# Gathering and spreading the routed tokens in two fp32r passes, with the gates multiplied in later and two low parts made on GpSimd

## The reference

```python
gate_out = x @ gate_w + routing_bias
top_v, top_i = jax.lax.top_k(gate_out, K)                 # K = 4 of E = 16
chosen = jax.nn.one_hot(top_i, E, dtype=x.dtype).sum(axis=-2)
probs = jax.nn.softmax(jnp.where(chosen > 0, gate_out, NEG), axis=-1)
weights = probs * chosen
out = _swiglu(x, sw1, sw2, sw3)                            # a = x@w1; silu(a) * (x@w2) @ w3
for e in range(E):
    out = out + _swiglu(x, w1[e], w2[e], w3[e]) * weights[..., e:e + 1]
```

## Time and profile before

| what | value |
|---|---|
| median of three runs | 502.1 us |
| time of the profiled execution | 502.08 us |
| its span, first to last instruction | 500.3 us (1.8 us lie around it) |
| granted TensorE clock | 0.99 of full |
| PE busy | 483.9 us, 97% |
| VectorE, ScalarE, GpSimd busy | 272.4, 205.5 and 9.1 us |
| DMA | 191.05 MB, mean 382 GB/s; the large queue took 96.0% of the 16 engines' span |

### The profile page before, as it was taken

One profiled execution on the slowest core, in us unless ns is written; L12 is line 12 of the kernel. 1 busy time (PEld: TensorE's weight loads), 2 busy tenths in 40 slices (PEclk: granted clock), 3 DMA queues, 4 the chain that ended last, 5 costly groups with the idle time before them and its releaser, 6 DMA issues.

```text
span 500.3 us, 6706 instructions
## 1 busy us (share of the span) xinstructions
PE 483.9 (97%) x2596; PEld 309.9 (62%) x2596; DVE 272.4 (54%) x326; ACT 205.5 (41%) x227; POOL 9.1 (2%) x46
## 2 busy tenths in 40 slices
PE   8989799999999999999999999999999999999987
PEld 4755433447887666576666756656666676565554
DVE  6734530146889674466538357546555645753542
ACT  1110101035787264555435345455444535545320
POOL 2000000010100000000000000000000000000000
PEclk9989999999999899999999999999999999999999
DMA  8999999999986989999999999999999999999980
GB/s 335 422 420 421 423 419 420 417 419 409 414 357 232 374 279 351 412 417 400 373 417 416 356 417 415 374 404 417 415 364 415 416 363 417 415 398 373 418 327 23
DMA packets 37555, 191.05 MB, mean 382 GB/s; under 512 B 4218, under 2 KB 4602, under 8 KB 32148
## 3 DMA queue, kind: packets, MB, share of 16 engines
q1 hardware_dynamic: 37328, 190.48, 96.0%
q10 hardware_dynamic: 196, 0.14, 0.1%
HBM read 190.35 MB, written 0.26 MB: 381 GB/s over the span
## 4 chain that ended last, share of the span: by engine, by line
PE 84%; DMA 6%; DVE 6%; ACT 2%; issue 2%; POOL 0%; SPq 0%; ACTq 0%; DVEq 0%; POOLq 0%
PE ps L1712 15%; PE ps L1783 13%; PE ps L1726 13%; PE ps L1796 7%; PE ps L1716 7%; DMA w_raw<-in_w 6%; PE ps L1360 4%; PE ps L1524 3%; PE ps L1763 2%; PE ps L1553 2%; PE ps L1541 1%; PE ps L1353 1%; PE ps L1422 1%; PE ps L1438 1%; DVE s_lo L981 1%
## 5 line engine op out<-in xcount | busy, mean ns | idle before, releaser
L967 DVE TENSOR_TENSOR s_lo<-w_raw,s_hi 128x1365 fp32r<-128x1365 f32 x72 | 111.9, 1579 | 69.4 <-ACT s_hi L710 68.4
L710 ACT CAST s_hi<-w_raw 128x1365 fp32r<-128x1365 f32 x72 | 94.4, 1333 | 49.6 <-DMA w_raw<-in_w 48.1
L1712 PE MATMUL ps<-s_hi,xT_hi 128*128 128x512 f32 (+2 forms) x216 | 86.2, 399 | 2.1 <-DVE s_lo L967 2.1
L1712 PE MATMUL ps<-s_lo,xT_hi 128*128 128x512 f32 (+2 forms) x216 | 80.0, 372 | 0.0
L1726 PE MATMUL ps<-w_raw,exS 128*64 128x512 f32 x480 | 74.2, 455 | 0.0
L723 ACT CAST s_hi<-w_raw 128x1536 fp32r<-128x1536 f32 (+1 forms) x36 | 48.9, 1369 | 52.5 <-DMA w_raw<-in_w 51.8
L981 DVE TENSOR_TENSOR s_lo<-w_raw,s_hi 128x1536 fp32r<-128x1536 f32 (+1 forms) x36 | 57.7, 1619 | 2.3 <-ACT s_hi L723 2.0
L1726 PEld LDWEIGHTS ps<-w_raw,exS 128*64 128x64 f32 x480 | 33.2, 136 | 40.0 <-issue 40.0
L1716 PE MATMUL ps<-s_hi,xT_lo 128*128 128x512 f32 (+2 forms) x216 | 57.0, 372 | 0.0
L1712 PEld LDWEIGHTS ps<-s_hi,xT_hi 128*128 128x128 f32 x216 | 41.0, 190 | 21.4 <-issue 11.8
L1712 PEld LDWEIGHTS ps<-s_lo,xT_hi 128*128 128x128 f32 x216 | 41.1, 190 | 8.3 <-issue 1.9
(11 more groups left out here) (296 smaller groups left out, 449.0 us busy)
## 6 DMA issues: line engine op xcount, KB each, us to landing
w_raw<-in_w SPq DMA_DIRECT2D x128, 682.5 KB, 12.0
w_set<-in_w SPq DMA_DIRECT2D x31, 1024.0 KB, 24.6
w_raw<-in_w SPq DMA_DIRECT2D x27, 768.0 KB, 11.8
w_raw<-in_w3s SPq DMA_DIRECT2D x24, 768.0 KB, 12.1
w_raw<-in_sw SPq DMA_DIRECT2D x8, 682.5 KB, 15.7
w_raw<-in_w SPq DMA_DIRECT2D x9, 512.0 KB, 12.2
wk_sb<-in_wk SPq DMA_DIRECT2D x2, 1024.0 KB, 16.8
wq_sb<-in_wq SPq DMA_DIRECT2D x2, 1024.0 KB, 16.0
```

The lines of the kernel that those rows point to most:

```text
L710: a.copy(s_hi[pair_of(g)][:, 0:F1], raw[:, 0:F1]).then_inc(hi_ready, 1)
L967: v.tensor_tensor(s_lo[pair][:, 0:F1], raw[:, 0:F1], s_hi[pair][:, 0:F1].bitcast(F32), ALU.subtract).then_inc(lo_ready, 1)
L1712: mm(bank(i + c0 // D)[:, 0:n], xT_hi[:, k], w[:, c0:c0 + n], start=(k == 0 and w is hi), stop=False)
```

## The change

The matrices of zeros and ones are held in fp32r. The gather takes the tokens in a high part (`rows_hi`, ScalarE) and a low part (`rows_lo`, GpSimd), two fp32r matmuls in place of one of float32, and all four gathers stand after the third piece of w2. `plan_gates` is gone: `spread` is plain zeros and ones, a small set of matmuls (`gates_of_slots`) puts the gate of each place into a column, and the gating of a few step multiplies by it. A result `y` is added in a high and a low part (`y_to_hi` on ScalarE, `y_to_lo` on VectorE). In step 1 VectorE makes the low part of w2's piece 0 ahead of the plan, GpSimd those of pieces 1 and 2, VectorE that of piece 3 after the plan. The last few step keeps its float32 matmuls.

```diff
@@ gpsimd
+            def lo_of_w2(k):
+                g = unit_w2(1, k)
+                pool.wait_ge(hi_ready, g + 1)
+                pool.wait_ge(lo_ready, g)
+                hi, lo = s_hi[pair_of(g)], s_lo[pair_of(g)]
+                pg.tensor_tensor(lo[:, 0:F1], w2_raw[k][:, 0:F1], hi[:, 0:F1].bitcast(F32), ALU.subtract).then_inc(lo_ready, 1)
+
+            pool.wait_ge(rows_ready, 2)
+            pg.tensor_tensor(rows_lo[:], xn[:], rows_hi[:].bitcast(F32), ALU.subtract).then_inc(rows_ready, 1)
+            lo_of_w2(1)
+            lo_of_w2(2)
@@ scalar
+            def copy_gate_slot():
+                act.wait_ge(round_ps, KT + 3)
+                a.copy(gate_slot[:], bank(7)[:, 0:len(SPARSE)]).then_inc(gate_slot_ready, 1)
+
+            def y_to_hi(e):
+                act.wait_ge(raw_used, few_of[e, 2, W3_UNITS - 1] + 1)
+                if few_no(e) > 0:
+                    act.wait_ge(added, few_no(e))
+                a.copy(y_hi[:], bank(7)).then_inc(y_hi_ready, 1)
...
             a.activation(xn[:], x3[:], ACT.Copy, scale=rstd[:]).then_inc(rows_ready, 1)
+            act.wait_ge(rows_ready, 1)
+            a.copy(rows_hi[:], xn[:]).then_inc(rows_ready, 1)
             hT_to_hi(0, 2)
             hi_w2(1, 0)
             hi_w2(1, 1)
             silu(1)
             hi_w2(1, 2)
-            copy_gathered(0)
-            copy_gathered(1)
             hi_w2(1, 3)
-            copy_gathered(2)
-            copy_gathered(3)
+            for k in range(KT):
+                copy_gathered(k)
...
                     hi_w2(m, 2)
+                    y_to_hi(m - 1)
                     hi_w2(m, 3)
...
                         copy_spread(1)
+                        copy_gate_slot()
@@ vector
-                v.tensor_tensor(rows, act_a[:, 0:CW], few_row(NC), ALU.mult).then_inc(h_ready, 1)
-                v.tensor_copy(y_sb[:], bank(7)).then_inc(y_few_ready, 1)
+                v.scalar_tensor_tensor(rows, act_a[:, 0:CW], gate_slot[:, few_no(e):few_no(e) + 1], few_row(NC), ALU.mult, ALU.mult).then_inc(h_ready, 1)
+            def y_to_lo(e):
+                dve.wait_ge(y_hi_ready, few_no(e) + 1)
+                v.tensor_tensor(y_lo[:], bank(7), y_hi[:].bitcast(F32), ALU.subtract).then_inc(y_few_ready, 1)
...
             hT_to_lo(0, 2)
+            lo_w2(1, 0)
             plan_order()
             routed_gates()
-            lo_w2(1, 0)
-            lo_w2(1, 1)
             plan_tokens()
-            lo_w2(1, 2)
+            dve.wait_ge(lo_ready, unit_w2(1, 3))
             lo_w2(1, 3)
-            plan_gates()
...
-                    copy_y(m - 1)
                     lo_w2(m, 2)
+                    y_to_lo(m - 1)
                     lo_w2(m, 3)
@@ tensor
-                mm(bank(6), spread[:, few_no(e)], y_sb[:], start=False, stop=False, skip_group_check=True).then_inc(added, 1)
+                mm(bank(6), spread[:, few_no(e)], y_hi[:], start=False, stop=False, skip_group_check=True)
+                mm(bank(6), spread[:, few_no(e)], y_lo[:], start=False, stop=False, skip_group_check=True).then_inc(added, 1)
...
-                    pe.wait_ge(rows_ready, 1)
+                    pe.wait_ge(rows_ready, 3)
...
-                mm(gathered[k], xn[:, P * k:P * k + P], hots[:].rearrange("p q n -> p (q n)"), start=True, stop=True).then_inc(round_ps, 1)
+                all_hots = hots[:].rearrange("p q n -> p (q n)")
+                mm(gathered[k], rows_hi[:, P * k:P * k + P], all_hots, start=True, stop=False)
+                mm(gathered[k], rows_lo[:, P * k:P * k + P], all_hots, start=False, stop=True).then_inc(round_ps, 1)
...
+            def gates_of_slots():
+                pe.wait_ge(round_ready, KT + 2)
+                for q in range(len(SPARSE)):
+                    for g in range(HALVES):
+                        last = mm(bank(7)[FEW * g:FEW * g + FEW, q:q + 1], hots[:, q].bitcast(F32), gate_at[:, BUSY + q:BUSY + q + 1],
+                                  start=True, stop=True, skip_group_check=True)
...
-                    if m == 2 and u in (0, 2):
-                        spread_few(u // 2)
+                    if m == 2 and u in (0, 1):
+                        spread_few(u)
+                    if m == 2 and u == 3:
+                        gates_of_slots()
...
-                    if m == 1 and k in (1, 2):
-                        gather_few(2 * k - 2)
-                        gather_few(2 * k - 1)
+                    if m == 1 and k == 2:
+                        for i in range(KT):
+                            gather_few(i)
```

More of the change, by code:

```diff
@@ L152, in gps_kernel @@
     exS = c("exS", [P, KT, len(SPARSE) * FEW])
-    spread = c("spread", [P, len(SPARSE), P])
-    hots = c("hots", [P, len(SPARSE), FEW])
-    gates = c("gates", [P, len(SPARSE), FEW])
+    spread = c("spread", [P, len(SPARSE), P], F32R)
+    hots = c("hots", [P, len(SPARSE), FEW], F32R)
+    y_lo = c("y_lo", [P, D], F32R)
     hS = c("hS", [P, S_TILES, P])
     hTS = c("hTS", [P, S_TILES, P])
-    y_sb = c("y_sb", [P, D])
+    y_hi = c("y_hi", [P, D], F32R)
+    rows_hi, rows_lo = y_hi, y_lo
+    y_last = hS[:].rearrange("p t n -> p (t n)")[:, 0:D]
+    gate_slot = c("gate_slot", [P, len(SPARSE)])
     table_in = c("table_in", [P, 2, E1])
@@ L347, in gps_kernel @@
     gate0_ps, max0_ready, exp0_ready, probs_ready = sem("gate0_ps"), sem("max0_ready"), sem("exp0_ready"), sem("probs_ready")
-    probs_bc, rank_seq = sem("probs_bc"), sem("rank_seq")
+    probs_bc, y_hi_ready = sem("probs_bc"), sem("y_hi_ready")
     poly_ps, poly_ready = sem("poly_ps"), sem("poly_ready")
@@ L365, in gps_kernel @@
     chosen_ready, counts_ps, counts_ready, table_ready = (sem(n) for n in ("chosen_ready", "counts_ps", "counts_ready", "table_ready"))
-    rows_ready, hots_ready, gates_ready, round_ps, round_ready = (sem(n) for n in ("rows_ready", "hots_ready", "gates_ready", "round_ps", "round_ready"))
+    rows_ready, hots_ready, gate_slot_ready, round_ps, round_ready = (sem(n) for n in ("rows_ready", "hots_ready", "gate_slot_ready", "round_ps", "round_ready"))
     hT_ps, hT_hi_ready, hT_lo_ready = sem("hT_ps"), sem("hT_hi_ready"), sem("hT_lo_ready")
@@ L1172, in gated_few @@
                 rows = hS[:].rearrange("p t n -> p (t n)")[:, 0:CW]
-                v.tensor_tensor(rows, act_a[:, 0:CW], few_row(NC), ALU.mult).then_inc(h_ready, 1)
[L1175 to L1179, removed]
-                v.tensor_copy(y_sb[:], bank(7)).then_inc(y_few_ready, 1)
+                if few_no(e) == 0:
+                    dve.wait_ge(gate_slot_ready, 1)
+                v.scalar_tensor_tensor(rows, act_a[:, 0:CW], gate_slot[:, few_no(e):few_no(e) + 1], few_row(NC), ALU.mult, ALU.mult).then_inc(h_ready, 1)
+            def y_to_lo(e):
+                dve.wait_ge(y_hi_ready, few_no(e) + 1)
+                v.tensor_tensor(y_lo[:], bank(7), y_hi[:].bitcast(F32), ALU.subtract).then_inc(y_few_ready, 1)
             def hT_to_lo(e, c):
@@ L1247, in plan_tokens @@
                                        position_at[:].unsqueeze(2).to_broadcast(each), ALU.add, ALU.is_equal).then_inc(hots_ready, 1)
[L1249 to L1253, removed]
             lo_w2(0, 0)
@@ L1315, in _ @@
             rows = hS[:].rearrange("p t n -> p (t n)")[:, 0:CW]
-            v.tensor_tensor(rows[:, 0:D], act_a[:, 0:D], few_row(NC)[:, 0:D], ALU.mult).then_inc(h_ready, 1)
+            gate = gate_slot[:, few_no(last):few_no(last) + 1]
+            v.scalar_tensor_tensor(rows[:, 0:D], act_a[:, 0:D], gate, few_row(NC)[:, 0:D], ALU.mult, ALU.mult).then_inc(h_ready, 1)
             dve.wait_ge(raw_used, few_of[last, 1, KT - 1] + 1)
-            v.tensor_tensor(rows[:, D:], act_a[:, D:CW], few_row(NC)[:, D:CW], ALU.mult).then_inc(h_ready, 1)
+            v.scalar_tensor_tensor(rows[:, D:], act_a[:, D:CW], gate, few_row(NC)[:, D:CW], ALU.mult, ALU.mult).then_inc(h_ready, 1)
             for b in range(2):
@@ L1322, in _ @@
                     dve.wait_ge(added, few_no(last))
-                v.tensor_copy(y_sb[:, HALF[b]], last_halves[b]).then_inc(y_few_ready, 1)
+                v.tensor_copy(y_last[:, HALF[b]], last_halves[b]).then_inc(y_few_ready, 1)
             dve.wait_ge(x3_ready, 1)
@@ L1789, in down_few @@
                 if u == 0:
-                    pe.wait_ge(y_few_ready, few_no(e)) if few_no(e) > 0 else pe.wait_ge(round_ready, KT + 2)
+                    pe.wait_ge(y_few_ready, few_no(e)) if few_no(e) > 0 else pe.wait_ge(gate_slot_ready, 1)
                 for i in range(3 * u, 3 * u + 3):
@@ L1813, in gather_few @@
                     pe.wait_ge(counts_ready, 1)
-                    pe.wait_ge(rows_ready, 1)
+                    pe.wait_ge(rows_ready, 3)
                     pe.wait_ge(hots_ready, 1)
                     pe.wait_ge(act_ready, 2)
-                mm(gathered[k], xn[:, P * k:P * k + P], hots[:].rearrange("p q n -> p (q n)"), start=True, stop=True).then_inc(round_ps, 1)
+                all_hots = hots[:].rearrange("p q n -> p (q n)")
```

(10 more changed lines are left out.)

## The result

| what | before | after |
|---|---|---|
| median (20 runs each, side by side) | 500.33 us | 501.92 us |
| ratio, 95% interval | | 1.0029 (1.0016 to 1.0042), or +1.45 us |
| profiled execution, its span | 502.08, 500.3 us | 501.36, 499.5 us |

The change made the kernel 0.3% slower. The profiled execution of before lies 1.75 us above the median of its 20 runs, so the two spans can't be set against each other; what follows compares single stretches. Part of the loss is in no stretch: the time around the span is 1.97 us in after's 20 runs (mean), where before has 1.77 to 1.78 in each of the four sets that were run beside the experiments. That is 0.2 of the 1.45 us; no run says why. A second profiled execution of before, unchanged, gave 500.0 us and a span of 498.2.

A forecast was written before the change was run, and what follows sets the result against it. The DMA's stream plus 26.4 us sets the end. The stream is 6.4 us late, less 3.2 us of idle time: 3.2 us late, span 503.5, with 1.8 us around it 505.3 us; range 497.5 to 508.

The forecast's parts named there:

- the table's delay: Step 1: the run-time table of experts ready at 169.0 us instead of 160.9, 8.1 us later.
- the stream of loads plus a fixed rest: Whole kernel: the end is the DMA's stream plus 26.4 us that the change doesn't shorten.
- The forecast's 26.4: Kernel's end: 26.4 us of casts, step 15's down projection, step 16 and output after the load landing at 473.85.
- TensorE's gains in the pairs: Adding the few results, seven times: PE gains 7 x 0.34 = 2.4 us, counted as 0 under the DMA.
- the forecast's 1.2: Step 1: GpSimd's subtraction of 512 elements a row for `rows_lo` takes 1.2 us.
- The first rival: Step 1: GpSimd runs beside VectorE, table 1.5 us later, 498.7 us; chance 0.30 shared with GpSimd behind the plan.
- the last (GpSimd behind the plan): Step 1: GpSimd starts its pieces after the plan, table at 162.4, about 499 us; chance 0.30 shared with GpSimd beside VectorE.
- the sum's terms ahead of the first load: Step 1, table: 160.9 + 1.5 (`lo_w2(1, 0)`) + 0.6 (`rows_lo`) + 6.0 (GpSimd's two low parts) = 169.0.
- the 3.2 us of idle time: DMA from 180 to 205 us: 349 GB/s against 401, 3.2 us lost, which the late stream swallows.
- That is hidden: TensorE's start of step 2 at 176.9 against 176.5, a us or two more if the clock falls: hidden.
- with the DMA's queue in front: Step 2 on PE: `gates_of_slots`, 16 float32 matmuls of one column, taken as 1.5 us, 0 on the end.
- The gather: Step 1 on PE: four float32 matmuls, 3.4 us, become eight fp32r ones, 2.1 us; step 2 at 176.9.

The follow-up runs named there:

- hots_later_22: Before, with only TensorE told of `hots` later, after a chain of 22 memsets on GpSimd: 1.0190 (1.0166 to 1.0213).
- dve_lows: After, with the low parts of w2's pieces 1 and 2 back on VectorE in before's order: 0.9993 (0.9976 to 1.0011).
- pool_after_table: After, with GpSimd waiting for the table to be ready ahead of its two low parts: 1.0022 (1.0006 to 1.0038).
- lows_then_tokens: After, all low parts on VectorE: piece 0, `plan_order`, pieces 1 and 2, `routed_gates`, `plan_tokens`, piece 3: 0.9981 (0.9962 to 1.0000).
- write_only: After, with GpSimd filling its two low parts with zeros by memsets instead of subtracting, their share of the product left out: 0.9942 (0.9921 to 0.9964).
- table_later_8: Before, with only SyncE told of the table later, after 8 short memsets on GpSimd: 1.0020 (0.9999 to 1.0041).
- both_later: Before, with SyncE told of the table after 32 memsets on GpSimd and TensorE of `hots` after 11 more: 1.0185 (1.0165 to 1.0206).

## Why the prediction was right or wrong

Forecast 505.3 us, +3.2 us over before; measured 501.92 us, +1.45. The direction and what GpSimd does to the plan were right. The size was more than twice too large: the table's delay was put at 8.1 us where it was 6.8, and the step from there to the end, with TensorE hidden behind the DMA, was wrong.

*Right.* The end is the stream of loads plus a fixed rest: from the landing of w3's last load of step 15 to the end it is 499.5 - 474.3 = 25.2 us, in before 500.3 - 475.1 = 25.2. (The forecast's 26.4 counts from 473.85, the landing of the load ahead of it; nothing hangs on the difference.) TensorE's gains in the pairs are real, 0.4 us each, and don't show in the time. GpSimd and VectorE exclude each other in both directions, a whole instruction at a time, where VectorE's has two SBUF inputs and GpSimd reads. GpSimd's long reads went first twice: 3.13 - 0.42 = 2.7 and 2.75 - 0.41 = 2.3 us of standing. The other way round, `rows_lo` came up at 154.75 inside a subtraction on VectorE that ended at 152.10 + 3.42 = 155.52, and ended 1.17 us after that, the forecast's 1.2. So the rule of the Trainium skill, SBUF — State Buffer, section Who interferes with whom, agrees with this trace. GpSimd's piece took 3.2 us, forecast 3.0. The first rival (both engines side by side) and the last (GpSimd behind the plan) are refuted by the same rows.

*The step that failed, first: the sum's terms ahead of the first load.* The forecast put the table 8.1 us late, it was 6.8. GpSimd's two pieces were counted whole, 6.0 us; they cost 5.0, since the copy, `order_key`, the memset and the reduction ran beside them or ahead of them. `lo_w2(1, 0)`, 1.57 us, and what `rows_lo` held up (L1011 took 1.73 us, 1.22 in before) came as forecast, and VectorE was 0.3 us earlier at this place than in before (156.04 against 156.30).

*Second, and the larger one in kind: "From there on every load's buffer is free before its turn, so the 3.2 us of idle time are swallowed", and of TensorE's start of step 2 "That is hidden".* What the table may be late is not the idle time of one window: it is the distance between two paths. In before it is 219.9 - 214.4 = 5.5 us, where the forecast had 1.7 (8.1 to 6.4 at the eighth load) + 3.2 = 4.9. With 6.7 us at the first load's landing and 5.5 to spare, 1.2 are left; L came 1.1 us later and the time 1.45, of which 0.2 lie outside the span. The error of 2 us at L is thus 1.4 from the table and 0.6 from the allowance. That the two allowances lie so close is luck: the forecast's 3.2 us of idle time and the distance of the paths are different things, and hots_later_22 shows it, where TensorE alone was late and the time rose by 9.5 us. And TensorE's start is not hidden but the other path: it set L in before, and S moved by 0.6 us in after, with `gates_of_slots` (1.10 us at 193.6) on the way, which the forecast counted at nothing "with the DMA's queue in front". Where TensorE leads, L - S is 43.4 to 44.1 us in the three kernels that have these matmuls and 42.3 to 43.8 in those that don't; so TensorE's path in after ends between 220.5 and 221.2, the table's at 221.1. They tie, or nearly; that `gates_of_slots` is what lengthens TensorE's is read from these rows, not tried. The tie fits dve_lows, which only came back to before (L 220.1).

*The gather.* The forecast had step 2 at 176.9; it was 177.08, which is luck: `hots` came 1.3 us sooner than forecast (171.4), and behind TensorE's wait of 3.15 us for it the clock fell (0.73 granted from 170 to 175), so that gather and piece 3 took 5.4 us instead of 4.2. Nor did all waits before it go: TensorE stood 1.15 us for GpSimd's low part of piece 2.

*Left open.* pool_after_table has L at 220.0, as before (219.9), and is 0.2% slower all the same; the two paths don't explain it. The times of the kernels that gain spread more than their landings, too: against the mean of before's two (219.6) lows_then_tokens has L 2.4 us ahead and is 0.9 us faster, write_only 2.1 us ahead and 2.9 faster, table_later_8 1.1 ahead and not faster at all. Some of it is the time around the span, 1.77 us in before but 1.99 in pool_after_table, 2.12 in lows_then_tokens and dve_lows, 2.21 in table_later_8 and 2.24 in write_only. For the rest, L is from one execution and the time from many, so no row says why. Whether the two passes for the few results are worth anything is below what was measured.

## What to carry to other kernels

Where a full DMA queue sets the end, find every path that leads to its filling: here the program's table (SyncE can't issue before it) and TensorE (buffers come free behind it), and write each as a start plus a fixed distance, from rows; only the later one counts (both_later and hots_later_22 cost the same), so mending the other wins nothing, and where two tie, both have to be mended. Work moved to GpSimd "beside" a chain of short VectorE operations with two SBUF inputs went in front of it here, a piece at a time, in all five traces that had it; the order of VectorE's own work was worth more here than the second engine.

## What was not expected of the hardware

- Which VectorE operations stand while GpSimd reads: `ahead` and `at_place`, with two SBUF inputs, did (2.7 and 2.3 us), the reduction at 163.36 (0.42 us, one SBUF input) didn't. But two inputs aren't what it takes: in pool_after_table `plain`, a TENSOR_SCALAR of 16 elements with one tile in and a column of another as its scalar, stood 2.66 - 0.23 = 2.4 us. GpSimd's writes let the two-input ones pass, while `plain` took 0.90 us beside one.
- The loads stumble at intervals. In before, two loads issued 0.5 us apart landed 3.2 us apart (199.0 + 7.4 and 199.5 + 10.2 us), while the stream's step is 1.7:

```profile
L482 SPq DMA_DIRECT2D w_raw<-in_w x1: 333/333/333, 199.0 to 199.0; - x1
DMA to landing us min/median/max: 7.4/7.4/7.4
...
L482 SPq DMA_DIRECT2D w_raw<-in_w x1: 541/541/541, 199.5 to 199.5; - x1
DMA to landing us min/median/max: 10.2/10.2/10.2
```

  In that stretch the view of the DMA queues from 206.5 to 209.5 us has one packet of the instruction queue:

```profile
q8 instruction: 1, 0.02, 2.1%
```

  It took 2.1% of 16 engines' 3 us, or 1.0 us of one engine. Such packets come every 24 us on average in the long stretch of all the kernels (14 to 29 us apart); that they are what delays the load beside them was only read from their place, not tried.
